# Down projection of the big expert blocks in three single-pass products, earlier requests for token rows, and a single-pass slot count

## The reference

```python
x = x + self_attention(layernorm(x), W_qkv, W_out)             # 16 heads of 16, causal, window 64
x = x + cross_attention(layernorm(x), ctx, Wq, Wkv, Wo, bias)   # 375 context rows, bias by distance
xf = layernorm(x).reshape(32 * 112, 256)
probs = softmax(xf @ router_w.T)                               # 8 experts
topv, topi = top_k(probs, 2)                                   # probs kept at the two best, renormalised
g = einsum('nd,edf->nef', xf, gate_w) + gate_b                 # d = 256, f = 512
u = einsum('nd,edf->nef', xf, up_w) + up_b
expert_out = einsum('nef,efd->ned', silu(g) * u, down_w) + down_b
x = x + einsum('ne,ned->nd', probs, expert_out)
```

## Time and profile before

| what | value |
|---|---|
| median of 3 runs | 1232.04 us (1231.17 to 1233.16) |
| profiled execution | 1233.23 us, span of the trace 1231.5 us |
| granted TensorE clock | 0.988 |
| PE / PEld busy | 1180.0 us (96%) / 1028.8 us (84%) |
| DVE / ACT / POOL busy | 881.8 us (72%) / 753.4 us (61%) / 824.4 us (67%) |
| attention part | start to about 885 us |
| change-over and 21 big pairs | about 885 to 1099 us |
| 21 small blocks and the end | about 1099 us to the end |

### The profile page before, as it was taken

One profiled execution on the slowest core, in us unless ns is written; L12 is line 12 of the kernel. 1 busy time (PEld: TensorE's weight loads), 2 busy tenths in 40 slices (PEclk: granted clock), 3 DMA queues, 4 the chain that ended last, 5 costly groups with the idle time before them and its releaser, 6 DMA issues.

```text
span 1231.5 us, 37033 instructions
## 1 busy us (share of the span) xinstructions
PE 1180.0 (96%) x12938; PEld 1028.8 (84%) x12938; DVE 881.8 (72%) x3849; ACT 753.4 (61%) x1847; POOL 824.4 (67%) x1594
## 2 busy tenths in 40 slices
PE   6899999999999999999999999999699999999996
PEld 4688888888888888888888888888499999999995
DVE  3567888878888788888887888888768655544442
ACT  3466766666666666666666666666475555545552
POOL 4577777777777877777877777776546645455332
PEclk8899999999999999999999999999999999999998
DMA  9311112111112211111211112112666433333321
GB/s 187 79 51 50 49 53 70 58 57 57 51 49 67 65 50 59 56 50 52 71 59 57 57 50 66 46 59 65 222 212 150 86 53 53 61 62 54 51 31 23
DMA packets 70937, 86.13 MB, mean 70 GB/s; under 512 B 25600, under 2 KB 57728, under 8 KB 70752
## 3 DMA queue, kind: packets, MB, share of 16 engines
q1 hardware_dynamic: 54768, 58.60, 16.5%
q0 software_dynamic: 15552, 25.05, 10.3%
q10 hardware_dynamic: 432, 0.10, 0.0%
HBM read 43.10 MB, written 20.95 MB: 52 GB/s over the span
## 4 chain that ended last, share of the span: by engine, by line
PE 89%; DVE 3%; issue 2%; ACT 2%; DMA 2%; POOL 1%; POOLq 0%; DVEq 0%; ACTq 0%
PE bank_S L885 10%; PE bank_Q L808 7%; PE bank_P L808 6%; PE bank_Q L900 6%; PE bank_S L799 5%; PE bank_S L850 5%; PE bank_B L821 4%; PE bank_A L821 3%; PE bank_A L788 3%; PE bank_A L721 3%; PE bank_B L721 3%; PE bank_B L788 3%; PE bank_B L780 3%; PE bank_A L780 3%; PE bank_A L729 3%; PE bank_Q L860 3%
## 5 line engine op out<-in xcount | busy, mean ns | idle before, releaser
L627 POOL TENSOR_SCALAR arena<-arena,mC 112x375 f32<-112x375 f32 x512 | 299.7, 598 | 55.5 <-DVE mC L1265 51.2
L1265 DVE CUSTOM_DVE_ANT_0 arena<-bank_S,arena 112x375 f32<-112x375 f32 x512 | 260.0, 542 | 44.6 <-PE bank_P L808 26.8
L633 POOL TENSOR_SCALAR arena<-arena 112x112 f32<-112x112 f32 x512 | 174.8, 360 | 83.5 <-DVE arena L1253 83.5
L653 POOL DMA_INDIRECT out<-y,xb x63 | 107.1, 1700 | 156.5 <-DVE y L1402 123.9
L808 PE MATMUL bank_Q<-ident,arena 112*126 112x112 f32 x858 | 132.6, 263 | 9.7 <-ACT pTC L1054 8.6
L1054 ACT ACTIVATE pTC<-bank_P 126x336 f32<-126x336 f32 x226 | 102.2, 452 | 40.5 <-PE bank_P L808 16.8
L808 PEld LDWEIGHTS bank_Q<-ident,arena 112*126 112x126 f32 x858 | 93.7, 140 | 30.2 <-ACT pTC L1054 19.7
L1253 DVE CUSTOM_DVE_ANT_0 arena<-bank_S,arena 112x112 f32<-112x112 f32 x512 | 102.1, 270 | 14.7 <-PE bank_S L738 14.7
L808 PE MATMUL bank_P<-ident,arena 112*126 112x112 f32 x678 | 107.7, 267 | 1.3 <-ACT pTC L1054 0.8
L1054 ACT ACTIVATE pTC<-bank_Q 126x336 f32<-126x336 f32 x222 | 100.9, 455 | 11.2 <-PE bank_Q L808 7.5
L808 PEld LDWEIGHTS bank_P<-ident,arena 112*126 112x126 f32 x678 | 74.5, 140 | 26.2 <-issue 16.1
(11 more groups left out here) (262 smaller groups left out, 3572.6 us busy)
## 6 DMA issues: line engine op xcount, KB each, us to landing
arena<-in_l_ctxT SPq DMA_DIRECT2D x32, 378.0 KB, 3.5
k<-k_low SPq DMA_DIRECT2D x64, 188.0 KB, 2.3
xb<-xs POOLq DMA_DIRECT2D x63, 129.0 KB, 3.5
q<-q SPq DMA_DIRECT2D x64, 112.0 KB, 2.2
arena<-in_L_ffn_gate_w SPq DMA_DIRECT2D x8, 512.0 KB
arena<-in_L_ffn_up_w SPq DMA_DIRECT2D x8, 512.0 KB
arena<-in_L_ffn_down_w SPq DMA_DIRECT2D x8, 512.0 KB
arena<-in_x SPq DMA_DIRECT2D x32, 112.0 KB, 2.0
```

Of the source, the lines that this page charges most:

```text
L627: pool.tensor_scalar(z[n % NZ][:, 0:T], z[n % NZ][:, 0:T], -1.0, mC[:, n:n + 1], ALU.mult, ALU.add).then_inc(s_u, 1)
L633: m = pool.tensor_scalar(sF[r][:, j, :], sF[r][:, j, :], -1.0, mF[:, r, j:j + 1], ALU.mult, ALU.add)
L653: pool.indirect_dma_start(out=out[:, :], out_offset=bass.IndirectOffsetOnAxis(ap=xb[x][:, D + 1:D + 2].bitcast(I32), axis=0), in_=y2[x % 2 ...
L1265: dve.tensor_tensor_reduce(out=z[n % NZ][:, 0:T], in0=bank[f"S{r}"][0:S, 0:T], in1=nbias[:, n, :], scale=1.0, scalar=3.0e38, op0=ALU.add, ...
```

## The change

The down product of a big pair is done in three passes as well: ACT makes `dwR_high` and `hR_high`, DVE `dwR_low` and `hR_low`, and PE runs 2 x 4 x 3 = 24 fp32r matmuls in the place of 8 fp32 ones. There is one `hidden_rows` buffer in the place of two, and the row buffers are 10, not 12. POOL asks for the rows of the next two blocks ahead of a pair's two adds, behind a wait for the adds of the pair before. The two slot products take fp32r operands: `before` is loaded into `x2[1]` and copied once, `ones` is made on DVE. In the hand-written order, `pfD` stands ahead of `blocks:2`, the first requests (`get`) stand among the last `u` steps, `bt` (the first pair's transposes) comes after `pv3`, the transposes of pair 1 come behind `bg:0`, and in each `bg` step DVE weighs the rows first.

```diff
-XB = 12
+XB = 10
@@ TAIL_ORDER
-e2 p13:-1 t7 p12:-1 e13:-1 t6 u7 e12:-1 p3 t5 pf:-3 u6 e3 t4 blocks:2 pv3:-1 u1 pfD:-3 S2 u4 oc3:-1 p0 u5 e0 t8
+e2 p13:-1 t7 p12:-1 e13:-1 t6 u7 e12:-1 p3 t5 pf:-3 u6 e3 t4 pv3:-1 u1 pfD:-3 blocks:2 S2 u4 oc3:-1 p0 u5 e0 t8
...
-p15 e14 warm pv2 oc1 e15 p13 oc2 p12 e13 pf:-2 e12 pkg:10 pkg:11 pkg:12 pkg:13 pkg:14 pkg:15 bt pfD:-2 rcB:-2
-x3T:-1 x3Tc:-1 pv3 oc3 bg:0 otc nrmc rt:-1 lg:-1 re:-1 sc:-2 bu:0 rcA:-1 onC oncc bg:1 woc st x2 ln3 rs3 pf:-1
+pv2 oc1 e15 p13 oc2 p12 e13 pf:-2 e12 pkg:10 pkg:11 pkg:12 pkg:13 pkg:14 pkg:15 pfD:-2 rcB:-2 x3T:-1 x3Tc:-1 pv3
+oc3 bt otc nrmc rt:-1 lg:-1 re:-1 sc:-2 bg:0 bt:1 onC oncc rcA:-1 bu:0 woc bg:1 st x2 ln3 rs3 pf:-1 pfD:-1
...
-                  for w, n, m in (("gw", DC, F), ("uw", DC, F))}
+                  for w, n, m in (("gw", DC, F), ("uw", DC, F), ("dw", FC, D))}
+            hR = [sb(f"hR_{part}", [P, FC, 2 * P], F32R, st) for part in ("high", "low")]
-            hidden_rows = [s1(f"hidden_rows{i}", [P, FC, 2 * P]) for i in range(2)]
+            hidden_rows = s1("hidden_rows", [P, FC, 2 * P])
-            before = s1("before", [S, S])
-            ones = s1("ones", [S, P])
+            before_in = x2[1][:, 0:S]
+            before = s1("before", [S, S], F32R)
+            ones = s1("ones", [S, P], F32R)
-            chosen = s1("chosen", [S, E])
+            chosen = s1("chosen", [S, E], F32R)
@@ POOL
+                    def load_pair(j):
+                        if j:
+                            pool.wait_ge(s_add, 16 * j)
+                        for n in (j + XB - 2, j + XB - 1):
+                            tables_ready(n)
+                            load(n, n % XB)
                     def add_and_load(j):
+                        if j < NFULL and j % 2 == 0:
+                            load_pair(j)
+                        if j >= NFULL:
+                            tables_ready(j + XB - 2)
                         add(j, j % XB)
-                        if j + XB - 2 < NBLK:
+                        if j >= NFULL and j + XB - 2 < NBLK:
                             load(j + XB - 2, (j - 2) % XB)
@@ PE
                     def down_pair(k):
-                        e = expert_of(pe, 2 * k)
-                        pe.wait_ge(s_hh, 2 * k + 2)
+                        pe.wait_ge(s_dw, k + 1)
+                        pe.wait_ge(s_hl, k + 1)
                         if k:
                             pe.wait_ge(s_yw, 2 * k)
-                        w = package(e, "dw").rearrange("p (c d) -> p c d", c=FC)
                         for h in range(2):
                             for c in range(FC):
-                                m = pe.matmul(bankY[:, h * D:(h + 1) * D], hidden_rows[k % 2][:, c, h * P:(h + 1) * P], w[:, c, :],
-                                              start=(c == 0), stop=(c == FC - 1))
+                                for u, w in PASSES:
+                                    m = pe.matmul(bankY[:, h * D:(h + 1) * D], hR[u][:, c, h * P:(h + 1) * P],
+                                                  wR["dw"][w][:, c, :], start=(c == 0 and (u, w) == PASSES[0]),
+                                                  stop=(c == FC - 1 and (u, w) == PASSES[-1]))
                             m.then_inc(s_y, 1)
@@ ACT
+                    def hidden_high(k):
+                        act.wait_ge(s_hh, 2 * k + 2)
+                        if k:
+                            act.wait_ge(s_y, 2 * k)
+                        act.activation(hR[0][:, :, :], hidden_rows[:, :, :], ACT.Copy).then_inc(s_hi, 1)
                         elif step == "bg":
                             weights_high(b, "uw", s_u2)
...
+                            if b:
+                                hidden_high(b - 1)
                             for half in range(2):
                                 silu_pair(b, half)
                         elif step == "bu":
+                            if b:
+                                weights_high(b - 1, "dw", s_y)
@@ DVE
+                    def hidden_low(k):
+                        dve.wait_ge(s_hi, k + 1)
+                        dve.tensor_tensor(hR[1][:, :, :], hidden_rows[:, :, :], hR[0][:, :, :].bitcast(F32),
+                                          ALU.subtract).then_inc(s_hl, 1)
                         elif step == "bg":
-                            weights_low(b, "uw", s_uw, 2)
-                            if b + 1 < NP:
-                                copy_low(b + 1)
                             if b >= 2:
                                 weigh_pair(b - 2)
+                            weights_low(b, "uw", s_uw, 2)
+                            if 0 < b < NP - 1:
+                                copy_low(b + 1)
+                            if b:
+                                hidden_low(b - 1)
                         elif step == "bu":
+                            if b:
+                                weights_low(b - 1, "dw", s_dw, 1)
```

More of the change, by code:

```diff
@@ L826, in slots @@
                         if b == 0:
[L827 removed]
+                            pe.wait_ge(s_pad0, 1)
                         need(pe, s_ex, b + 1)
@@ L1102, in weights_high @@
                             act.wait_ge(used, 2 * k)
-                        act.activation(wR[part][0][:, :, :], package(e, part).rearrange("p (c f) -> p c f", c=DC), ACT.Copy).then_inc(s_wh[part], 1)
+                        act.activation(wR[part][0][:, :, :], package(e, part).rearrange("p (c f) -> p c f", f=parts[part][1] // (
+                            FC if part == "dw" else DC)), ACT.Copy).then_inc(s_wh[part], 1)
                     def silu_pair(k, half):
@@ L1312, in set_up @@
                         link(dve.memset(pad[:, :], 0.0))
+                        link(dve.tensor_scalar(ones[:, :], pad[0:S, 0:P], 1.0, None, ALU.add))
                         link(dve.tensor_copy(rowf[:, :], rowid[:, :]))
```

65 lines of the change are left out of this document (39 added, 26 removed).

## The result

The changed kernel takes 1246.0 us (median of 4 runs, 1240.98 to 1247.74) where the kernel before takes 1231.6; the ratio is 1.0103 with a 95% interval of 1.0077 to 1.013. It is slower by 14.4 us between the medians and by 12.7 us (9.5 to 16) by the ratio, and lies above the range of the prediction (1226.5 to 1239). Span of the profile: 1245.0 us against 1231.5, at a clock of 0.986 against 0.988.

What follows compares the result with a forecast made beforehand. PE was taken to bound the big pairs; 1233.23 - 3.7 + 1.3 + 3.0 - 0.6 + 0.8 = 1234.0 us, with the median 1.2 lower at 1232.9, no measurable change; range 1226.5 to 1239.

Steps and rivals of the forecast that it cites:

- The down product itself: Down in big pairs: 24 fp32r matmuls take 2.88 us in place of 3.45, saving 0.57 us a pair.
- The stall in front of down in an even pair: Even pairs: PE waits 0.76 us for the down weights' split; net +0.19 us a pair, +3.0 us over 16.
- Requests ahead of the adds: POOL in the expert part: the new wait leaves time for two requests; 0 us, from -0.5 to +1.
- the last down's -0.6 us: Down of pair 20: a small block's gate and up cover its splits, so it changes by -0.57 us.
- Pairs 0 to 4 give it back: First pairs: waits before down use up the earlier start of gate 0; both together +1.3 us, -3 to +4.
- Clock: Waits of 2 to 3 us ahead of down 0, 1 and 2 may lower PE's clock: +0.8 us, up to 3.
- Change-over: Start of the expert part: gate 0 starts earlier, a lead of 3.4 us (1 to 5).
- Slots: Slot products on PE: 0.12 us saved in each of 31 sequences, -3.7 us (0 to -6).
- Rival (b): Whole kernel slower: the chain of splits is longer and the clock falls, 1238.6 us; chance 0.31.

Runs made afterwards that it cites:

- a_old_requests: Changed kernel with the old order of adds and requests on POOL, without the wait for the adds of the pair before; ratio 1.0088 to the kernel before.
- a_early_12_seam: Changed kernel with old order of requests, 12 row buffers, earlier split of the down weights and changed hand-over to the small blocks; ratio 0.9953 to the kernel before.
- a_early: Changed kernel with the down weights split earlier on ACT and DVE, all else as changed; ratio 1.0075 to the kernel before.
- b_new_requests: Kernel before with the new order of requests and adds on POOL alone, still 12 row buffers; ratio 1.0057 to the kernel before.
- before_again: Kernel before, unchanged, profiled once more beside the experiments; 1222.9 us.
- one_pass_down: Changed kernel with the down product of the big pairs and its operands as before, all else as changed; ratio 0.9964 to the kernel before.

## Why the prediction was wrong, step by step

- **The down product itself: right.** At the higher clock 24 matmuls take 2.86 to 2.98 us (2.88 forecast).
- **The stall in front of down in an even pair: right.** A pair of 9.79 us where I had 9.64 + 0.19; PE's idle time in front of down is 0.47 us in the records, which overlap by 0.16 us, so down starts 0.63 us late (0.68 forecast). T6-T20 is +3.9 us; a_old_requests, without the ring, has +2.5 against 14 x 0.19 = 2.7, and the other 1.4 come with the requests.
- **"Requests ahead of the adds ... nothing gained or lost: 0, from -0.5 to +1": this step failed.** I counted POOL's work, 5.29 of 9.65 us, and found room. But the new wait ties it into a ring with the adds: from the start of the second add to its landing 3.8 to 4.7 us pass, and POOL stands idle for 3.4 to 4.5 us ahead of the next request. A round takes 9.6 to 10.5 us, as long as a pair or longer. Alone the new order costs 7.0 us, put into a_early_12_seam 14 us. At the hand-over, where I had only the last down's -0.6 us, I found +7.5, of which the old order takes 3.8 away. My first theory after the result, that it lengthens every pair to 10.4, was wrong as well.
- **"Pairs 0 to 4 give it back": this sum failed too.** The change-over and these pairs were to be +1.3 us together (-3 to +4); from S26 to T6 it is +9.1. Down 0 was to start 10.1 us after `gwR_low` of pair 1 (893.18); it starts 13.5 us after it. The 3.4 us over are DVE's idle time ahead of `x2` (3.41 us), a wait that the sum put at nothing. a_early, which moves only the split, takes 5 to 7 us away.
- **Clock (+0.8, one more stretch up to 3 us): mis-sized.** Down 0, 1 and 2 stood behind waits of 5.96, 1.74 and 2.08 us and all three ran in good part at 1.2 GHz: 4.8 us more than in a_early, at a granted clock of 0.82, 0.87 and 0.88.
- **Change-over (lead 3.4, 1 to 5): right.** Counted from S26, gate 0 starts 3.0 us earlier (at 884.46, before at 894.13), up to 0.8 of it from four shorter sequences.
- **Slots: mis-sized to the good side**, 0.20 us a sequence for 0.12. The products themselves are 0.12 us shorter, as forecast; the period is 0.20 shorter.
- **Rival (b)** had the right sign, and the clock is part of it; but its chain of splits was no longer than forecast, and the requests are not in it.

Sum of what happened: -6.7 - 2.7 + 11.8 + 3.9 + 7.5 - 0.3 = +13.5 us. Not settled is how the requests' part and the splits' part divide inside the changed kernel, since they don't add up: three passes taken out, 16 us go; requests taken out, 1 to 9; the split moved, 3 by the ratio and 5 to 7 by the profile.

## What to carry to other kernels

Before an engine is given a wait for its own earlier transfer, add up the whole ring (issue, landing, what stands between), not the engine's busy time: a ring as long as the loop costs nothing inside the loop until something else gets faster, and can still hold up what comes behind it (b_new_requests: 5.2 us at the hand-over). A product that needs split operands gains only if each split starts as soon as its inputs stand; look for small steps and table steps in front of it, above all at a change of phase, and for idle time that the engine with the split will have there. Count such a wait of PE higher than its length: here the products behind waits of 1.7 to 6 us ran in good part at the lower clock. And measure the edits in pairs: here the costs of two edits were far from the sum of each alone.

## What the runs showed of the hardware

- The attention part has two period lengths 0.50 us apart. The kernel before took 26.7 us for each sequence in its first profile, and 26.17 or 26.67 in before_again; S26 is at 801.62 in the one and at 790.38 in the other, which is more than the 7 us between the sets. In the set in which the kernel before took 1231.1 us, the profiles of the changed kernels show the longer period (26.49) almost everywhere. What chooses between them stays open.
- From the start of its issue to its landing the second indirect add of a pair took 3.7 to 3.9 us in one_pass_down, 3.7 to 4.5 in b_new_requests and 3.8 to 4.7 in the changed kernel, for rows of the same size; 1.6 to 2.5 us of it are POOL's issue. The first two both have the fp32 down product and 878 us of DVE's work (925 in the changed kernel), so neither the three passes nor DVE's sum explains the difference. It stays open.
- The granted clock fell to 0.82 to 0.88 in pairs 1 to 3 of the changed kernel, where PE waited 1.7 to 6 us in front of each down product; behind the waits of 0.47 us in the even stretch it stayed at 1.00.
- One fp32r slot product of 8 columns takes 0.10 us from start to start.
